# A fused two-attention, two-MoE kernel: the router norms' square roots leave GpSimd, and nine shared pieces instead of ten run ahead of the first expert chunk

## The reference

```python
x = x + attn_a(layernorm(x))   # one head of 128, no mask
x = x + ffn(layernorm(x))      # router, top 2 of 8 experts, capacity 1280, plus 0.1 * shared expert
x = x + attn_b(layernorm(x))   # 16 heads of 8, causal
x = x + ffn(layernorm(x))
# layernorm: (x - mean) / sqrt(var + 1e-5)
```

## Time and profile before

| | |
|---|---|
| median of three runs | 774.4 us |
| the profiled execution's own time | 779.2 us |
| its span in the trace | 777.5 us |
| busy share PE / PEld / DVE / ACT / POOL | 91 / 83 / 68 / 58 / 58 % |
| DVE busy between 60 and 80 us (first attention) | 15.59 of 20 us |
| POOL busy between 60 and 80 us | 15.63 of 20 us |
| PE busy between 200 and 240 us (expert layer 0) | 40.00 of 40 us |

### The profile page before, as it was taken

One profiled execution on the slowest core, in us unless ns is written; L12 is line 12 of the kernel. 1 busy time (PEld: TensorE's weight loads), 2 busy tenths in 40 slices (PEclk: granted clock), 3 DMA queues, 4 the chain that ended last, 5 costly groups with the idle time before them and its releaser, 6 DMA issues. The chain is left out here.

```text
span 777.5 us, 18451 instructions
## 1 busy us (share of the span) xinstructions
PE 708.2 (91%) x6152; PEld 643.6 (83%) x6152; DVE 525.9 (68%) x1665; ACT 449.7 (58%) x1144; POOL 454.4 (58%) x564
## 2 busy tenths in 40 slices
PE   6888789699999997888999998999999899999996
PEld 5777689699999995666777776777779799999996
DVE  5877775366556555867888989877777356665536
ACT  2566454244444443676878878787755344446545
POOL 7367777166666662334545776777767166666650
PEclk9999989899999998899999999999999899999999
DMA  7997111455556335233433444323101346555318
GB/s 252 313 317 171 45 48 55 57 109 109 103 98 129 80 96 135 92 98 109 148 90 98 124 124 140 94 92 121 53 30 52 50 75 135 110 92 114 91 60 290
DMA packets 167718, 89.38 MB, mean 115 GB/s; under 512 B 120576, under 2 KB 151890, under 8 KB 167528
## 3 DMA queue, kind: packets, MB, share of 16 engines
q1 hardware_dynamic: 156792, 70.02, 36.3%
q0 software_dynamic: 9216, 17.34, 6.6%
q10 hardware_dynamic: 1616, 0.84, 0.6%
HBM read 49.63 MB, written 39.67 MB: 115 GB/s over the span
## 5 line engine op out<-in xcount | busy, mean ns | idle before, releaser
L1289 ACT ACTIVATE hT<-bank,bias_T 128x256 f32<-128x256 f32 x448 | 175.7, 475 | 193.5 <-PE bank L917 193.4
L624 POOL DMA_INDIRECT y_rows<-yo,row_cur x160 | 168.7, 1054 | 124.3 <-DVE yo L1828 88.9
L1934 DVE TENSOR_REDUCE negp<-bank 128x2 f32<-128x512 f32 (+1 forms) x192 | 129.6, 685 | 45.6 <-PE bank L979 27.2
L938 PE MATMUL bank<-w_s,hT 128*128 128x128 f32 x1280 | 156.0, 275 | 0.0
L609 POOL DMA_INDIRECT x_slots<-xr,slot_u x128 | 131.4, 1026 | 41.6 <-issue 34.3
L938 PEld LDWEIGHTS bank<-w_s,hT 128*128 128x128 f32 x1280 | 150.0, 192 | 0.0
L917 PE MATMUL bank<-xT_hl,w_hl 128*128 128x256 f32 x960 | 136.5, 292 | 10.8 <-DVE xT_hl L1702 10.7
L693 POOL TENSOR_SCALAR_AFFINE_SELECT pt<-pt 128x512 f32<-128x512 f32 x128 | 86.0, 680 | 92.6 <-ACT pt L1372 92.3
L917 PEld LDWEIGHTS bank<-xT_hl,w_hl 128*128 128x128 f32 x960 | 122.0, 194 | 13.2 <-issue 11.6
L1372 ACT ACTIVATE pt<-bank 128x512 f32<-128x512 f32 x192 | 107.8, 596 | 40.6 <-PE bank L1000 38.7
L1828 DVE TENSOR_TENSOR yo<-bank,b_b 128x256 f32<-128x256 f32 x80 | 34.0, 425 | 103.8 <-PE bank L938 102.2
(11 more groups left out here) (214 smaller groups left out, 1209.4 us busy)
## 6 DMA issues: line engine op xcount, KB each, us to landing
xg_all<-x_slots SPq DMA_DIRECT2D x320, 32.0 KB
w_s<-in_L_ffn_w SPq DMA_DIRECT2D x32, 256.0 KB
qk_rows<-qks SPq DMA_DIRECT2D x16, 512.0 KB, 3.9
bdk<-qk_rows SPq DMA_DIRECT2D x187, 32.0 KB
qc<-qk_rows SPq DMA_DIRECT2D x45, 128.0 KB, 2.9
x_slots<-xg_all SPq DMA_DIRECT2D x1, 5440.0 KB, 21.2
y_rows<-xg_all SPq DMA_DIRECT2D x1, 4096.0 KB, 14.3
yab<-y_rows SPq DMA_DIRECT2D x16, 256.0 KB, 3.5
```

The lines of the kernel that those rows point to most:

```text
L624: pool.indirect_dma_start(y_rows, bass.IndirectOffsetOnAxis(ap=row_cur[:, g % ROWS, j:j + 1], axis=0), yo[:, g % RING, j, :], None, bounds ...
L938: m = pe.matmul(yb(w, l)[:, j * P:(j + 1) * P], hT[:, w % 2, f, j * P:(j + 1) * P], wt[:, f, :], start=(f == 0), stop=(f == FT - 1))
L1289: a = act.activation(hT[:, w % 2, f, :], HB[2 * (w % 2) + f // 2][:, (f % 2) * 256:(f % 2) * 256 + 256], ACT.Silu, bias=bias_T[:, b0 + f:b ...
L1934: dve.tensor_reduce(dst, AB[(g + k) % 2][:, :].rearrange("p (j k) -> p j k", j=heads), AX.X, ALU.max, negate=True).then_inc(S.amax_done, 1)
```

## The change

- In the first attention the router norms' roots leave GpSimd. ScalarE computes log(var + eps) and exp(-0.5 * that) (`root_guess(n)`), and VectorE one Newton step on it in three scalar_tensor_tensor instructions (`root_of(n, 0..2)`). The first attention's other roots (line 564, 566) and all roots of the second attention stay on GpSimd.
- GpSimd's hand-written interleaving goes: it sends rows 0 to 63 in a plain loop, held only by the waits inside `dispatch`.
- `FRONT` for layer 0 goes from 10 to 9; seven shared pieces instead of six follow the chunks.
- Small additions: a constant column of eps, written by VectorE at the start, four semaphores, and changed counts on `ln2_ve`.

```diff
-FRONT = (10, 10)
+FRONT = (9, 10)
...
@@ GpSimd, attn_a
-                for q in range(2, 7):
+                for q in range(2, 8):
                     rstd_of(q, q + 1)
-                rstd2_of(1)
-                rstd_of(7, 8)
-                rstd2_of(2)
...
-                for i in range(2, PAIRS):
-                    n = 2 * i
-                    if i > 2:
-                        pool.wait_ge(S.probs_tr, n + 1)
-                        row()
-                        pool.wait_ge(S.gv_done, min(n + 3, SEQS))
-                        row()
-                    pool.wait_ge(S.y_done, n + 1)
-                    row()
...
-                    rstd2_of(i + 1)
-
-                for k in range(k, 2 * NT):
+                for k in range(2 * NT):
                     dispatch(0, k)
@@ ScalarE
+            def root_guess(n):
+
+                act.wait_ge(S.ln2_mv, n)
+                need(act, S.ln2_rstd, n - 1)
+                act.activation(var_log[:, :], mv2[:, :, 1], ACT.Ln, bias=eps_col[:, 0:1]).then_inc(S.var_log, 1)
+                act.wait_ge(S.var_log, n)
+                act.activation(seed[:, :], var_log[:, :], ACT.Exp, scale=-0.5).then_inc(S.root_seed, 1)
...
                 if 0 <= n + 2 < SEQS:
                     g_copy(n + 2)
+                if valid(i - 1):
+                    root_guess(i)
                 if 0 <= n + 1 < SEQS:
                     exps(n + 1)
...
+            root_guess(PAIRS)
             act.activation(bq_s[:, :], bias_T[:, 36:37], ACT.Copy, scale=HD ** -0.5)
@@ VectorE
+            def root_of(n, k):
+
+                if k == 0:
+                    dve.wait_ge(S.root_seed, n)
+                    need(dve, S.ln2_rstd, n - 1)
+                    dve.scalar_tensor_tensor(out=root_t[:, 0, :], in0=seed[:, :], scalar=-0.5, in1=seed[:, :], op0=ALU.mult, op1=ALU.mult
+                                             ).then_inc(S.root_step, 1)
+                elif k == 1:
+                    dve.wait_ge(S.root_step, 2 * n - 1)
+                    dve.scalar_tensor_tensor(out=root_t[:, 1, :], in0=mv2[:, :, 1], scalar=EPS, in1=root_t[:, 0, :], op0=ALU.add, op1=ALU.mult
+                                             ).then_inc(S.root_step, 1)
+                else:
+                    dve.wait_ge(S.root_step, 2 * n)
+                    need(dve, S.xn2_ready, n - 1)
+                    dve.scalar_tensor_tensor(out=rstd2[:, :], in0=root_t[:, 1, :], scalar=1.5, in1=seed[:, :], op0=ALU.add, op1=ALU.mult
+                                             ).then_inc(S.ln2_rstd, 1)
...
                 if 0 <= n + 1 < SEQS:
                     maxes(n + 1)
+                if led:
+                    root_of(i, 0)
                 if valid(i):
                     add_attn(n)
+                if led:
+                    root_of(i, 1)
                 for j in range(PLACED):
                     if routed:
                         placed(i - 2, j, bank[2])
+                    if led and j == 0:
+                        root_of(i, 2)
                     if led and j < 4:
                         norm_r(i - 1, j)
...
                     if l == 0 and w == 0:
+                        for k in range(3):
+                            root_of(PAIRS, k)
                         for j in range(4):
                             norm_r(last, j)
```

More of the change, by code:

```diff
@@ L168, in build @@
         on = sb("on", [P, 2, HEADS, HD]); onT = sb("onT", [P, SEQ]); osum = sb("osum", [P, 2, HEADS])
+        eps_col = sb("eps_col", [P, 1], F32)
+        var_log = sb("var_log", [P, 4], F32)
+        seed = sb("seed", [P, 4], F32)
+        root_t = sb("root_t", [P, 2, 4], F32)
         x_cols = sb("x_cols", [P, 2, CH * P])
@@ L253, in build @@
         S.xg_used = sem("xg_used")
+        S.eps_set = sem("eps_set")
+        S.var_log = sem("var_log")
+        S.root_seed = sem("root_seed")
+        S.root_step = sem("root_step")
         S.row_set = sem("row_set")
@@ L586, in rstd2_of @@
                 pool.wait_ge(S.ln2_mv, n)
-                if n > PAIRS + 1:
-                    pool.wait_ge(S.xn2_ready, n - 1)
+                pool.wait_ge(S.xn2_ready, n - 1)
                 pool.tensor_scalar(ve2[:, :], mv2[:, :, 1], EPS, 1.0, ALU.add, ALU.mult).then_inc(S.ln2_ve, 1)
-                pool.wait_ge(S.ln2_ve, n)
+                pool.wait_ge(S.ln2_ve, n - PAIRS)
                 pool.tensor_tensor(rstd2[:, :], ve2[:, :], neg_half[:, :], ALU.pow).then_inc(S.ln2_rstd, 1)
@@ L1272, in attn_a_pair @@
                     xnT_copy(n + 4)
+            act.wait_ge(S.eps_set, 1)
             for i in range(-2, PAIRS):
@@ L1464, in _ @@
             dve.memset(mask_f[:, :], 0.0).then_inc(S.const_dve, 1)
+            dve.memset(eps_col[:, :], EPS).then_inc(S.eps_set, 1)
             dve.memset(xg_all[:, :], 0.0).then_inc(S.zero_set, 1)
```

## The result

The changed kernel takes 796.75 us (median of six runs, 794.83 to 799.47) against 775.21 us of the kernel before beside it: a ratio of 1.0277 [1.0251, 1.0304], 21.5 us slower. The forecast was 769.6 us. The profiled execution took 794.83 us, its span is 793.1 us. What happened is the mechanism of the rival with the table loads, and it cost more than that rival's 16.6 us.

The account below looks back on a forecast made before the run. TensorE, busy 91%, bounds the kernel; 9.5 us are lost at expert layer 0's first chunk. Attention +2.2, gap -4.6, clock -2.4 make -4.8 us, from a median of 774.4 to 769.6 us; range 766.8 to 774.5.

Parts of the forecast that it names:

- the rival with the table loads: Attention, ScalarE: Ln and Exp each need a load, VectorE waits 2.4 us a step; +16.6 us, 786.2 us, chance 0.10.
- I take no load, since both run without one if they are in one set: Attention, ScalarE: Ln and Exp cause no table load and fit, at 0.53 us, in its 0.75 us hole each step.
- one gap of 2.5 us: TensorE ahead of expert layer 0's first chunk: idle from 134.75 until the chunk is ready at 137.2.
- The step is a loop that goes through VectorE's work, and what is put between `lead` and `norm_r` lengthens every step: First attention: three new VectorE instructions lengthen each of seven steps by 0.36 us, 2.5 us in all.
- the term +2.2 us: The attention and everything after it come 2.2 us later; bounds 0 and 4.8 us.
- the second rival: The attention doesn't get longer, so the time is 767.4 us; chance 0.18.
- GpSimd's rows: Scatter rows at 1.26 to 1.32 us each keep up with the attention; the last ends near 129.6 instead of 135.2.
- the first rival: Clock falls in the 2.5 us gap before the first chunk, or VectorE pays 4.8 us: 772.0 us, chance 0.20.
- -4.8: Sum for what follows the first chunk: attention +2.2, gap -4.6, clock -2.4 us.
- 2.5 us is nearer the former: First chunk, TensorE: clock holds over 2.5 us idle, as after 1.79 us, unlike after 7.1 us; worth -2.4 us.
- FRONT 9: Expert layer 0: with nine pieces ahead of the first chunk, TensorE keeps a 2.5 us gap a tenth would have filled.

Follow-up runs that it names:

- the kernel with the loads alone: The kernel before, roots still on GpSimd, plus ScalarE's Ln and Exp for seven attention steps, result unused: 801.28 us, ratio 1.0332.
- the kernel with one set: The changed kernel plus one ScalarE instruction at the start loading the function set that holds both exp and ln: 772.93 us, ratio 0.9953.
- the kernel with one set and ten pieces: The changed kernel with the exp-and-ln function set loaded once at the start and ten shared pieces ahead of the chunks, not nine: 771.61 us, ratio 0.9925.
- the one with twelve matmuls: The changed kernel, loads included, plus twelve unread matmuls on TensorE ahead of the transposes of probs in each step: 792.97 us, ratio 1.0236.

## Why the prediction was wrong

**The step that failed: "I take no load, since both run without one if they are in one set."** The condition is right, and the step from it to this program was not. The trace of before has Copy and Exp running without a load between them, and the prediction did not ask which set they run in. Sixteen loads show that this set did not hold Ln, and that the set loaded for Ln was not kept for the next Exp; with the set of both loaded once at the start, there is none. The Trainium skill, "ScalarE: Activation LUTs", section "Table sets: the hidden batching unit", counts one load for ln and then exp, because one set has both. In the changed kernel that did not hold (two loads for each pair); after the set had been asked for by name it did. How the sets are chosen was not traced further than these two programs. The Trainium skill, "ScalarE: Activation LUTs", section "What ACT_TABLE_LOAD costs", gives 2.66 us for a switch with a drain; here it is 1.28 us, and Ln starts 0.01 us behind the load's end (55.55 + 1.28 to 56.84).

**The rival's price, 2.4 us a step and 16.6 us in all, was too small.** Its loads were priced right: 2.5 us a step measured with the clock held. Its place was wrong (VectorE's wait for the seed; the kernel with the loads alone has no such wait and the same step), and by coincidence the exps are late by the same 2.3 us. What it left out is TensorE's clock, 1.5 us a step in the middle, though the prediction had the rows to fear it: it priced a falling clock for one gap of 2.5 us and did not ask it of the gaps of 3.1 us that its own rival would make in the attention. Measured against before, the first `norm_r` comes 3.0 us later (33.40 against 30.37), the time from the first pair's norms to the last's grows by 22.4 us (95.46 instead of 73.02), and 1.1 us come behind them, where TensorE waits 2.44 us for the last norms and no longer 1.39. By root, the first six cost 21.8 us where the rival had 6 x 2.4 = 14.4, the seventh 2.4 where it had 0.9, and the eighth, with what follows it, 2.4 where it had 1.3. Together 26.6 us up to the ninth piece, where forecast and rival together had 2.2 + 16.6 = 18.8. For the chance of 0.10 the prediction gave nothing of the trace that spoke against the loads.

**"The step is a loop that goes through VectorE's work, and what is put between `lead` and `norm_r` lengthens every step"** was half right. The loop goes through VectorE up to the reduction ahead of the exps. The three new instructions stand behind it, where 0.3 to 0.4 us are free. So a step grew by 0.05 us, not 0.36, and the term +2.2 us was 0.1 to 0.5: in the kernel with one set the last `norm_r` starts at 103.90 instead of 103.39, the ninth piece at 129.47 instead of 129.34. (With ten pieces the same attention had its last `norm_r` at 103.97, and the ninth piece at 131.47, because the clock was at 0.50 for the first two pieces, 2.90 and 2.91 us.) What misled was reading "no gap on VectorE" as "on the path": the engine was busy all along, but TensorE's product came from its own earlier wait for probs, 0.85 us in that step. This was the second rival's outcome; its 767.4 us did not come, because TensorE then arrived 2.1 us sooner than forecast (129.47 + 3.21 = 132.68 instead of 134.75) at a chunk that came only 0.7 us sooner.

**GpSimd's rows** were forecast well, with a little luck. They cost 1.28 us each, mostly, where 1.26 to 1.32 was taken, but the last sixteen cost 1.36 ((128.70 - 108.26) / 15 in the kernel with one set). That the last starts at 128.70 (forecast: near 129.6) and the chunk is ready at 136.54 (137.2) is this and an attention that did not grow by 2.2. No run has the plain loop with the roots still on GpSimd, or the other way round, so what each of the two brought is open.

**The gap and the clock.** Without the loads the gap was 3.60 us and the clock at 0.50 behind it: the first rival's mechanism, through a longer gap than it had. In the prediction's own terms the gap is 136.54 - 132.68 = 3.9 us. By the trace that makes +0.1 for the attention, 3.9 - 7.1 = -3.2 for the gap and +0.1 for the clock, together -3.0 us, by the ratio -3.6, instead of -4.8. In the changed kernel the gap was 1.86 us, and the clock held. The step "2.5 us is nearer the former" took one short gap for the rule. A few microseconds further down, at the attention's end, the same trace spoke against it:

```profile
94.94 1.87 PE L830 MATMUL bank<-router,xnT_all 128*128 128x8 f32 x8 [0.69 <-ACT xnT_all L1239]
96.67 2.06 PE L810 MATMUL bank<-v_s,pT 128*128 128x128 f32 x8
99.93 2.90 PE L917 MATMUL bank<-xT_hl,sw_hl 128*128 128x256 f32 x12 [1.21 <-issue]
```

The router product takes 1.03 us in the steps before and the product with v 1.06 to 1.14; here both are slow, and so are the twelve matmuls of the first shared piece. The clock was 1.00 up to 93, 0.74 from 93 to 94 and 0.50 from 94 to 102. It fell without any wait longer than the 1.79 us at 89.33, while TensorE was busy for 2.97 of the 6 us from 88 to 94.

**FRONT 9.** The prediction said that a gap stays "which a tenth piece would have filled". With the tenth piece the kernel with one set went from 0.9953 to 0.9925, and the clock held. In the kernel before, nine pieces cost 0.5%. The intervals of the first two overlap, so the gain itself rests on the traces.

## What to carry to other kernels

Before a function is added on ScalarE, ask which set of functions the neighbours run in, not only whether some set holds them all; if one does, load it by name ahead of the first, and look for ACT_TABLE_LOAD in the first profile. To find the loop of a software pipeline, put a small idle copy at two places of one engine and compare the step lengths: a busy engine without gaps can still have slack, and a third of a microsecond decides where a few instructions are free. Price a stall of TensorE's once with and once without the slow clock behind it, at every place where the stall recurs.

## What the runs showed of the hardware

How long TensorE stands idle doesn't by itself tell what the clock does. Twice the same wait ahead of the same matmuls ended at either level, in kernels that differ only elsewhere. An idle 2.25 us left it at 1.00 in the changed kernel and was followed by 0.50 in the one with twelve matmuls. An idle 1.88 us ahead of a product with v left it at 1.00 in the kernel with one set and ten pieces (1.13 us, at 89.59) and was followed by 0.50 in the one with nine (1.90 us, at 90.64). Of the changed kernel's six waits of 3.1 to 3.4 us for probs, the first and longest, 3.40 us, left it at 1.00 (transposes 0.66 and scores 1.03 us, at 33.33); with each of the other five it fell to 0.50, by the transposes or while the scores ran. The wait of 1.79 us left it at 1.00, and so did those of 1.86 us at the first chunk, in the changed kernel and in that with one set and ten pieces; with that of 3.60 us it fell. At the attention's end it fell with no wait longer than 1.79 us. Filled with matmuls that nothing reads, the stretch ahead of the transposes stayed at 1.00. The price of the falls in the attention was 1.5 us a step in the mean of four, against 2.4 us at the expert layer's first chunk.

A table load took 1.28 us each time, and the root's Ln or Exp behind it started 0.01 to 0.02 us after its end.
